# A four-layer sandwich kernel on one core: the exact three-way split of queries and keys moves from VectorE to GpSimd, the two norms at the input become one, and the order of the work is planned anew

## What is computed

```python
x = _ln(x, norm_in_g, norm_in_b) + pos_emb        # the caller passes _layernorm(x) in here
for l in range(LAYERS):
    q, k, v = ...                                  # 16 heads of 8
    attn = softmax(where(valid, q @ k / sqrt(8), neg)); o = attn @ v
    x = _ln(x + o @ Wo[l].T + bo[l], ...)
    x = _ln(x + gelu(x @ W1[l].T + b1[l]) @ W2[l].T + b2[l], ...)
```

## Time and profile before

| what | value |
|---|---|
| median of three runs | 1100.56 us (1100.5 to 1101.69) |
| span of the profiled execution, first to last instruction | 1102.7 us |
| TensorE matmul busy | 994.2 us, 90% |
| VectorE busy | 809.7 us, 73% |
| ScalarE busy | 763.1 us, 69% |
| GpSimd busy | 407.5 us, 37% |
| instructions | 47422, 20080 of them matmuls |

### The profile page before, as it was taken

How to read it: one execution, slowest core, us unless ns; L and a number is a source line. 1 busy time by engine, 2 the same in 40 slices (tenths; PEclk the granted TensorE clock), 3 DMA queues, 4 the chain that set the end, 5 groups by cost and what they waited for, 6 DMA issues and landing times.

```text
span 1102.7 us, 47422 instructions
## 1 busy us (share of the span) xinstructions
PE 994.2 (90%) x20080; PEld 705.4 (64%) x20080; DVE 809.7 (73%) x2451; ACT 763.1 (69%) x1418; POOL 407.5 (37%) x544
## 2 busy tenths in 40 slices
PE   1679999999999999999998999998987988899993
PEld 0356777777777777777775777666664544555772
DVE  6777887777778887777777775879798979872320
ACT  7457666767777667767773777767767868688741
POOL 8711433333344433333344213444646353401311
PEclk9769999999999999999998999999999989999997
DMA  5522211222225211332224123221112020401220
GB/s 160 116 62 61 61 42 42 78 70 61 62 62 105 56 43 41 64 89 62 61 62 103 27 38 61 60 46 29 35 28 60 3 61 4 117 26 37 68 77 10
DMA packets 72627, 64.80 MB, mean 59 GB/s; under 512 B 16226, under 2 KB 66914, under 8 KB 72418
## 3 DMA queue, kind: packets, MB, share of 16 engines
q1 hardware_dynamic: 72418, 61.78, 23.3%
HBM read 15.70 MB, written 1.05 MB: 15 GB/s over the span
## 4 chain that ended last, share of the span: by engine, by line
PE 72%; DVE 11%; ACT 5%; POOL 5%; issue 3%; SPq 1%; DMA 1%; POOLq 0%; DVEq 0%; ACTq 0%
PE b L775 11%; PE b L887 9%; PE b L878 8%; PE b L676 7%; PE b L756 5%; PE b L790 4%; PE b L959 4%; PE b L949 4%; PE b L709 4%; PE b L806 2%; PE b L846 2%; PE b L871 2%; DVE mx L1218 2%; ACT probs L1021 2%; PE b L862 2%
## 5 line engine op out<-in xcount | busy, mean ns | idle before, releaser
L1021 ACT ACTIVATE probs<-b 128x443 f32<-128x443 f32 (+2 forms) x736 | 354.0, 543 | 137.5 <-PE b L756 96.5
L1218 DVE TENSOR_REDUCE mx<-b 128x2 f32<-128x378 f32 (+1 forms) x768 | 353.0, 508 | 93.9 <-PE b L709 93.5
L676 PE MATMUL b<-band,identb 64*64 64x252 bf16 x2304 | 170.4, 286 | 18.4 <-DVE mx L1218 8.1
L775 PE MATMUL b<-probs,vals 128*32 128x189 f32 (+5 forms) x3968 | 182.8, 311 | 1.2 <-DVE mx L1218 0.3
L775 PEld LDWEIGHTS b<-probs,vals 128*32 128x32 f32 x3968 | 115.1, 110 | 47.2 <-issue 12.2
L1543 POOL TENSOR_SCALAR veps<-mv 128x4 f32<-128x4 f32 x48 | 11.0, 230 | 352.4 <-DVE mv L1324 352.4
L756 PE MATMUL b<-qpack,kpack 64*64 64x189 bf16 (+5 forms) x3968 | 137.0, 236 | 0.3 <-issue 0.3
L709 PE MATMUL b<-kpack,qpack 62*64 62x189 bf16 (+1 forms) x3072 | 122.0, 239 | 1.0 <-issue 1.0
L676 PEld LDWEIGHTS b<-band,identb 64*64 64x64 bf16 x2304 | 67.0, 105 | 83.6 <-issue 36.5
L887 PE MATMUL b<-w,hid 128*128 128x128 f32 x768 | 110.1, 287 | 0.0
L1215 DVE TENSOR_REDUCE mx<-b 128x1 f32<-128x512 f32 (+7 forms) x256 | 99.3, 444 | 14.1 <-PE b L724 13.7
(11 more groups left out here) (173 smaller groups left out, 1695.7 us busy)
## 6 DMA issues: line engine op xcount, KB each, us to landing
kpack<-kparts SPq DMA_DIRECT2D x168, 128.2 KB
qpack<-qparts SPq DMA_DIRECT2D x168, 128.0 KB, 3.4
qpack<-mrows SPq DMA_DIRECT2D x224, 4.0 KB
w<-in_w SPq DMA_DIRECT2D x12, 256.0 KB, 4.3
w<-in_wa SPq DMA_DIRECT2D x12, 256.0 KB, 3.3
w<-in_wb SPq DMA_DIRECT2D x12, 256.0 KB, 3.7
rowt<-in_rowt SPq DMA_DIRECT2D x6, 384.0 KB, 3.4
stream<-in_x SPq DMA_DIRECT2D x4, 256.0 KB, 4.0
```

The source lines that it names most:

```text
L676: pe.matmul(out, identb[rows, rows], rhs.unsqueeze(1).to_broadcast([64, 2, 2, EDGE]), start=True, stop=False, skip_group_check=True)
L775: mm = pe.matmul(bank("sum", u, group)[32 * j:32 * j + 32, q0:q0 + w - skip], vals[:, u % 2, at:at + 32], probs[:, n % SETS, j, col + skip ...
L1021: act.activation(probs[:, n % SETS, j, 0:width], bank("exp", u, v, b)[:, 0:width], ACT.Exp, scale=SCALE).then_inc(a_emptied, 1)
L1218: red = dve.tensor_reduce(out[:, 2 * tb:2 * tb + 2], read[:, 0:2 * width].rearrange("p (t k) -> p t k", k=width), AX.X, ALU.max)
```

## The change

It has seven parts.

1. `high` writes the full f32 value into `qrest` or `krest` and frees the bank itself; it waits only for the unit before to be split (`q_lo`, `k_lo`), no longer for its DMAs. `rests` on VectorE is gone. `lower` on GpSimd has four operations in place of two: round, subtract, round, subtract. GpSimd now makes the wait for the DMAs of the unit before. Only the first unit of a layer writes column 0 of the keys.
2. The keys of unit 0 are packed by ScalarE's queue, beside SyncE's, which packs the queries.
3. The norm k = 0 is left out, and k = 1 computes both in one: its variance v goes through v(1 + EPS) + EPS².
4. The clears of the three query and three key buffers are made in 32-bit words (half as many elements); `qpack` is one element longer so that it divides.
5. The semaphores are cleared by ranges of neighbouring numbers.
6. The planner counts TensorE's instructions: at each 256 the next page must have arrived, 3850 ns after the last crossing.
7. The planner's mode prices, slacks, `TURN_WORTH` (15422 to 0), `TABLE_WORTH` and all offsets have new values, so that the order on each engine is another one.

```diff
             def high(u, name):
...
+                full, lo = (qrest, q_lo) if name == "q" else (krest, k_lo)
...
                 if u:
-                    act.wait_ge(packed, u * PACKED)
-                act.wait_ge(d_filled, filled(name, u))
+                    act.wait_ge(lo, u)
+                act.wait_ge(a_filled, filled(name, u))
...
-                act.activation(parts[:, 0, first:], bank(name, u)[:, :], ACT.Identity, bias=bias
-                               ).then_inc(done, 1)
+                act.activation(full[:, first:], bank(name, u)[:, :], ACT.Identity, bias=bias).then_inc(a_emptied, 1)
...
+            def pack_first():
+                act.wait_ge(k_clean, 1)
+                act.wait_ge(k_lo, 1)
+                for r, n in enumerate(KROLES):
+                    act.dma_start(kpack[r:P:ROLE_STEP, 0, :, 0:HEADED], kparts[:, n, :]).then_inc(k_packed, 16)
...
-                dve.scalar_tensor_tensor(out=rest[:, first:], in0=bank(name, u)[:, :], scalar=bias,
-                                         in1=parts_[:, 0, first:], op0=ALU.add, op1=ALU.subtract
-                                         ).then_inc(d_emptied, 1)
...
             def lower(u, name):
...
+                if u:
+                    pool.wait_ge(packed, u * PACKED)
+                pool.wait_ge(a_emptied, emptied(name, u))
+                pool.tensor_copy(parts_[:, 0, cut], rest[:, cut]).then_inc(hi, 1)
+                pool.wait_ge(hi, u + 1)
+                pool.tensor_tensor(rest[:, cut], rest[:, cut], parts_[:, 0, cut], ALU.subtract).then_inc(left, 1)
+                pool.wait_ge(left, u + 1)
+                pool.tensor_copy(parts_[:, 1, cut], rest[:, cut]).then_inc(mid, 1)
                 pool.wait_ge(mid, u + 1)
+                pool.tensor_tensor(parts_[:, 2, cut], rest[:, cut], parts_[:, 1, cut], ALU.subtract).then_inc(lo, 1)
...
-            for s in semaphores:
-                pool.sem_clear(s)
+            for i, n in enumerate(numbers):
+                if i + 1 == len(numbers) or numbers[i + 1] != n + 1:
+                    pool.sem_clear(range(numbers[first], n + 1))
+                    first = i + 1
...
-    norm_jobs(plan, b, 0, ("x", b))
-    norm_jobs(plan, b, 1, ("nscale", b, 0))
+    norm_jobs(plan, b, 1, ("x", b))
...
+            if e == "pe":
+                n = fetched(name)
+                ahead = FETCHED - count % FETCHED
+                if n >= ahead:
+                    crossed = max(at + job.cost * ahead // n, arrives)
+                    job.end = crossed + job.cost - job.cost * ahead // n
+                    arrives = crossed + FETCH
+                count += n
...
-                    pool.memset(qpack[:, where[0], :], 0.0).then_inc(q_clean, 1)
+                    pool.memset(qpack[:, where[0], :].bitcast(F32), 0.0).then_inc(q_clean, 1)
```

More of the change, by code:

```diff
@@ L99 @@
 SAME = {"pe": 0, "dve": 118, "act": 120, "pool": 100, "sp": 0}
[L100 to L113, removed]
@@ L114 @@
[L114 to L121 removed]
+TURN = {"q": 200, "k": 200, "out": 205, "hid": 200, "ffn": 200, "mixin": 200, "mixv": 200, "ehid": 200, "eout": 200,
+        "cat": 152, "turn": 152, "norm": 152, "rows": 152, "weigh": 165, "v": 200, "phase": 200}
@@ new lines @@
+TURN_LEAST, TABLE_LOAD = 122, 1400
+FETCH, FETCHED, VLOADS = 3850, 256, 80
+TURN_WORTH = 0
+TABLE_WORTH = 442484
+SLACK = {"act": 454, "dve": 3, "pe": 41, "pool": 2726, "sp": 0}
+BIAS = {"active": -1151810, "add": 162712, "band": 128801, "blank": 169197, "bo": 40958, "bo_in": 253540, "cat":
+        3602573, "cnorm": 61834, "consts": 97281, "even": -680932, "exp": -1134028, "ffn": -940810, "gelu": -282112,
+        "heads": 55413, "hid": 1202026, "high": -103016, "ident": -37385, "in": -11462, "k": 1921, "kclean":
+        -186250, "later": 45513, "load": -592539, "lower": 779758, "masks": 332425, "max": 596, "maxrows": 87186,
+        "mrows": -144937, "norm": 856231, "ocat": 2196902, "odd": -710077, "out": 1251622, "pack": 1992568, "parts":
+        116, "place": -383254, "places": 35, "q": 1498132, "qclean": -1678544, "recip": 137308, "residue": 144863,
+        "root": -445619, "row": -353059, "scale": -2045715, "score": -1401, "shifts": -275624, "sin": -102319,
+        "split": -416765, "stats": -155805, "sum": -367492, "top": 481320, "turn": 2926400, "v": 1743, "weigh":
+        -1971221, "x": -789390}
@@ L125, with fetched @@
 CAP = {"exp": 3, "heads": 8, "hid": 3, "max": 8}
+def fetched(name):
+    kind, c = name[0], len(name) > 1 and isinstance(name[1], int) and causal(name[1])
+    if kind == "max":
+        return 16 * len(CAUSAL_TILES[name[3]]) if c else 24
+    if kind == "score":
+        return 16 * len(CAUSAL_BANKS[name[3]]) if c else 40
+    if kind == "weigh":
+        return 16 * len((CAUSAL_BANKS if c else CHUNK_BANKS)[name[3]])
+    if kind == "v":
+        return VLOADS - 16 * c
+    return {"q": 4, "k": 4, "phase": VLOADS - 16, "parts": 8, "turn": 8, "cat": 8, "out": 16, "norm": 8, "hid": 4, "ffn": 16,
+            "rows": 8, "mixin": 20, "mixv": 16, "router": 4, "logits": 4, "spread": 4, "ehid": 4, "eout": 16}[kind]
 class Job:
@@ L198, in arrange @@
         clock = {e: 0 for e in self.order}
+        count, arrives = 0, 0
         mode = {e: None for e in self.order}
@@ L280, in consumer @@
         return "sum"
-    if kind in ("exp", "parts", "cat", "norm", "hid", "rows", "mixr", "router", "ehid"):
+    if kind in ("q", "k", "exp", "parts", "cat", "norm", "hid", "rows", "mixr", "router", "ehid"):
         return "act"
@@ L505, in _ @@
         def _(pool):
-            for s in semaphores:
-                pool.sem_clear(s)
+            numbers = sorted(s.num for s in semaphores)
+            first = 0
+            for i, n in enumerate(numbers):
+                if i + 1 == len(numbers) or numbers[i + 1] != n + 1:
+                    pool.sem_clear(range(numbers[first], n + 1))
+                    first = i + 1
 def whole_phase(nc, env):
@@ L1184, in _ @@
                     clean_keys(*where)
+                elif kind == "pack":
+                    pack_first()
                 elif kind == "sin":
@@ L1475, in _ @@
                     parts(*where)
-                elif kind == "rest":
-                    which, u = where
-                    rests(u, which)
                 elif kind == "even":
```

77 lines of the change are left out of this document (38 added, 39 removed).

## The result

| what | before | changed |
|---|---|---|
| median of the runs of this comparison | 1101.12 us (1100.5 to 1104.06, 4 runs) | 1115.58 us (1113.99 to 1117.47, 4 runs) |
| span of the profiled execution | 1102.7 us | 1115.7 us |
| TensorE busy | 994.2 us | 1010.2 us |

The changed kernel is slower: the ratio is 1.0118, 95% interval 1.01 to 1.0136. 1079 had been forecast, in a range of 1062 to 1092, so the sign was wrong too.

What follows compares the result with a forecast made beforehand. TensorE was taken as the bound in the steady part and experts, with gains at the start, causal part, tail and order. -6.6 - 9 - 1 - 5 = -21.6 on the 1102.7 us span gave 1081, so a 1079 median; range 1062 to 1092.

Steps and rivals of the forecast that it cites:

- the moved split: Rests leave VectorE, two operations join GpSimd: covered by TensorE in the steady part, small causal-part gain; -1 us, bounds -6 and +6.
- the order: New engine lists, instruction fetch included: fill part of TensorE's idle time behind 93 us; -5 us, bounds -18 and +20.
- Range clears: Tail behind the last matmul: one clear, taken at 44 ns, replaces 91 single semaphore clears; -6.6 us.
- The start: First unit: earlier `state` and key issues, the latter 10.5 us earlier, of which 9 us counted; bounds 4 and 14.
- Contention: More two-input GpSimd work slows VectorE: 56 pairs, at most 1 us each, covered except eight in the causal part.
- The 1200 ns row: Row of the trace before: a 32-element VectorE operation of 193 ns once took 1200, cited as contention with GpSimd.
- The sign named for it: Sign that the forecast is wrong: TensorE busy grown by mode changes, meaning the new list changes tiles more often.
- slower: GpSimd's list: Rival: `lower` waits for DMAs in GpSimd's in-order list, so norm roots, scaling and hidden layer start late; chance 0.05.
- its threshold, 0.77 us a unit: In the slower rival: TensorE idle added per unit from which the 21.6 us saved over 28 units are lost.
- its 1107: In the slower rival: the time in us if TensorE idles 1 us more a unit, 1079 + 28.

Runs made afterwards that it cites:

- e3: Changed kernel's code with the old order and old split, keeping range clears, single norm, word-wide cleans and first keys on ScalarE's queue; 1095.81 us, ratio 0.9934.
- e12: Changed kernel with GpSimd's residues of two neighbouring norms exchanged at four places, nothing else; 1111.14 us, ratio 1.0052 to the kernel before.
- e13: e12 plus the light split of e11 (two subtractions of each split on 8 columns from unit 1 on); 1102.24 us, ratio 1.0.
- e2: Changed kernel's code with the engine lists and banks of the kernel before (old order, new split); 1153.18 us, ratio 1.0459.
- e4: Changed kernel's new order with the old split (high, rests on VectorE, two-operation lower on GpSimd); 1172.03 us, ratio 1.0627.
- e11: Changed kernel, lists untouched, with the two subtractions of each split cut to 8 columns from unit 1 on; 1119.26 us, ratio 1.0139.
- e5: e3 plus an unused rounding and an unused two-input operation on GpSimd behind each split, 3.3 us a unit; 1158.38 us, ratio 1.0545.

## Why the prediction was wrong

Two terms of the sum failed, the moved split at -1 and the order at -5, and with them the sign; the other two held in place and size. What stands in their place is told by stretches first. The 30.5 us between the end of the first hidden layer and the last matmul divide as follows. The 24th hidden layer, the last of the six layers, ends at 869.8 us before and 868.6 after.

| stretch | before | changed | e3 | e12 | e13 |
|---|---|---|---|---|---|
| to the end of the first hidden layer | 106.4 | 95.0 | 104.1 | 96.4 | 96.5 |
| from there to the end of the 24th | 763.4 | 773.6 | 763.2 | 767.3 | 760.7 |
| from there to the last matmul | 216.0 | 236.3 | 215.2 | 236.3 | 236.3 |
| behind it | 16.9 | 10.8 | 10.9 | 10.8 | 10.8 |

The second row is where the pairs of norms and the split's length act: 773.6 - 767.3 = 6.3 us go with the exchange (e12), which is a loss of the new order, and 767.3 - 760.7 = 6.6 more with the light split (e13). The rest, 30.5 - 12.9 = 17.6, stands in e13 too, and so is the new order's. It is 12.2 us more of busy TensorE behind the first hidden layer (940.6 beside 928.4) and 5.4 more of idle. The windows of the last stretch, before and changed:

```profile
869.80:1085.80 216.00, 202.77 (x2871) 123.54 (x2870) 124.27 (x430) 159.97 (x323) 60.02 (x113) 0.98 0.18 50
```

```profile
868.60:1104.90 236.30, 217.85 (x3194) 130.16 (x3192) 138.57 (x479) 166.60 (x344) 76.73 (x141) 0.98 0.21 53
```

The new list leaves 323 matmuls more for the end, 15.1 us of TensorE, and is idle for 18.5 us there instead of 13.2. Its middle stretch has 339 matmuls fewer (15565 beside 15904), so it should have been 15 us shorter than before; even e13's is only 2.7 shorter.

Whether the longer last stretch comes from the order or from the new split, e2 and e4 tell, which have one of the two each. The new split in the old order (e2), then the old split in the new order (e4):

```profile
919.90:1144.60 224.70, 206.59 (x2870) 125.06 (x2870) 123.32 (x426) 159.97 (x323) 67.04 (x121) 0.95 0.18 48
```

```profile
925.50:1163.20 237.70, 217.06 (x3195) 130.15 (x3193) 139.83 (x482) 166.61 (x345) 69.54 (x131) 0.99 0.20 50
```

The stretch goes with the order: 237.7 us in e4 beside 215.2 in e3 with the old split, and 236.3 in the changed kernel beside 224.7 in e2 with the new one.

Point by point, by the prediction's own steps:

- *Range clears, -6.6.* Right. 5 to 6 us in time; 10.8 us behind the last matmul instead of 16.9. The changed kernel has one range clear, and it took 0.55 us: more than the 44 ns of the low end, much less than the 6.7 us of the single ones.
- *The start, -9.* Right in mechanism, place and nearly in size: 11.4 us at the end of the first hidden layer. With the new order and the new split together it stands in the other traces too (e12 96.4, e13 96.5), and the stretches behind it lose more; with the old split it is gone (e4 118.2). In the old order it hardly arises, so no run shows whether it would have come through to the end by itself.
- *The moved split, -1 with bounds of -6 and +6.* This step failed. It was costed by GpSimd's busy share (176 of 496 us) and declared covered from 93 to 589 us by TensorE being full. Between a norm's `mv` and its matmul TensorE has next to no cover: the root, the scaling and the transpose are one chain, and the list in front of the root had room for 1.2 us a unit and not for 2.1. In the old order, whose rows the bounds were made from, the split costs 57 us. In the new order its length costs 6 to 9, or nothing as long as the pairs hide it.
- *Contention, inside the +6.* The 1200 ns row was read rightly, and its place wrongly. It was counted by the number of VectorE operations under the new GpSimd work. What matters is one operation on the chain of a norm, and in the new order it is an old GpSimd operation, the residue, that holds it, because two norms are now neighbours. The trace of before had the sign already: two of its 192 scalings, at 705.7 and 826.0 us, took 1251 and 1195 ns beside a median of 341, each beside a GpSimd operation with two inputs.
- *The clock* was in no term. Each of the changed kernel's four gaps of 2.5 us in the steady part was followed by matmuls at the lower level of the clock (1.2 GHz beside 2.4), so these gaps cost more than their length: the hidden layer's group is busy for 94.5 us instead of 89.7. Behind the first hidden layer TensorE is busy at the low level for 38.0 us, beside 14.9 before and 25.8 in e13. At half speed, an estimate, that is 11.6 us of the 18.4 that it is busier there.
- *The order, -5 with bounds of -18 and +20.* This step failed too, and it is wrong in sign: 17.6 us that e13 keeps, and the pairs' 6.3 besides. The bound for the loss was large enough, but not for its reason, steady stretches with more idle: in e13 TensorE is idle for 37.9 us of the middle stretch, as before (37.8), and what grew is its busy time and the idle of the last stretch. The sign named for it did come, in small: counted in the trace, TensorE changes its tile shape 926 times and did so 905 times. Of the 12.2 us more of busy TensorE in e13, 6.1 are in the projection of queries and keys (53.0 us busy behind the first hidden layer, 47.0 before). Twenty-six of its 96 matmuls there stand directly behind another tile shape and take 697 ns in the median, beside 592 for the others; nine did before (17 x 0.105 = 1.8 us). The low clock, by the 10.9 us more that TensorE is busy at it in e13, makes an estimated 5.4. The other 5 of the 12.2 are not settled.
- *Adding the two* was an error of its own. Either part alone is slower than both together (1153 and 1172 beside 1116), so neither has a price without the other. With both left out (e3) the rest of the change is faster than before. With the split lightened and the pairs taken apart (e13) the new order ends level with the kernel before: by itself it takes up all that the clears and the start bring.
- *The rival "slower: GpSimd's list"* had the mechanism of the old order exactly, root behind `lower`, scaling behind the root, matmul behind the scaling. There its threshold, 0.77 us a unit, was passed: 57 / 28 is 2.0. In the changed kernel it was not: the split's length is worth 6 to 9 us there, 0.3 a unit at most, and its 1107 came near the 1115.6 partly by luck, as most of the loss was the order's. It was given a chance of 0.05 because GpSimd was idle for most of the time.

Not shown is why the new order's late stretch is idle for 5.3 us more, and a root computed on VectorE, which would take GpSimd out of the chain, was not tried.

## What to carry to other kernels

Cost work that moves to an in-order engine by the gap in its list in front of the next operation that somebody waits for, not by its busy share. Here, on an engine idle for 64% of the time, 1.2 us more a unit were free within the noise, 2.1 cost 17 and 3.3 cost 61. Where two parts of a change are a data path and an order, run the four combinations before explaining either: the clears, the single norm and the start with the old order and the old split give 1095.8 us, which beats both kernels. And when the repair of one loss brings nothing, repair the second and try the first again: e11 alone brought nothing, behind e12 it brought 6 to 9 us.

## What the runs showed of the hardware that was not expected

- An f32 operation of VectorE from SBUF to SBUF that starts within 0.1 us of a GpSimd operation with two inputs, behind it or just ahead of it, lasts until that one ends: 1.27 and 1.42 us instead of 0.34 each, so 3.12 for the four. GpSimd's own operation is hardly longer (1.28 us beside 1.27). VectorE's reductions, which read PSUM, showed no such rows.
- The same waits of TensorE differ in price by what the clock does after them. The granted clock was 1.00 in the 31 us ahead of the gap of 2.47 us, 0.89 in the next 31, and 1.00 again behind them. The length of the gap does not decide it: of e5's ten waits for `ztok` of 2.2 to 2.6 us behind the first hidden layer, six were followed by the low level and four were not. The 10 us behind two waits of 2.51 us each:

```profile
203.60:213.60 10.00, 10.00 (x181) 6.91 (x182) 6.37 (x15) 8.59 (x13) 2.53 (x2) 1.00 0.30 57
304.80:314.80 10.00, 9.99 (x143) 6.54 (x144) 5.28 (x13) 7.42 (x11) 2.54 (x2) 0.83 0.25 57
```

- GpSimd is held up as well: in the fill two operations of `lower` took 1.48 and 0.95 us, where the same took 1.16 and 0.61 later. Two operations of VectorE with two inputs each (`place`) ran beside them.
